# One edge buffer, sixteen output slots and one step a turn in a graph-layer kernel

## The chip, the core and the metric

The kernel runs on one core of one Trainium2 chip. The metric is the device time of one execution in microseconds. Five engines share the work: TensorE (PE in the profile, its weight loads PEld), VectorE (DVE), ScalarE (ACT), GpSimd (POOL) and SyncE (SP), which here only issues DMA transfers. The profile page comes from one profiled execution.

## What is computed

A layer over a graph with 12,500 nodes of 128 features and 412,500 edges of 48 features. The edges are sorted by `dst`, the node that receives them.

```python
recv = edge_index[1]
agg = jax.ops.segment_sum(edges, recv, num_segments=N_NODES)
u = graph_globals[batch]                      # batch is all zeros
x = jnp.concatenate([nodes, agg, u], axis=1)  # nodes = relu(layernorm(x))
h = jax.nn.relu(x @ W1 + b1)                  # 256 hidden
return h @ W2 + b2                            # added to the layer's input x
```

Everything is float32. The edge features are 79 MB of the 88 MB that are read, and 6.4 MB are written.

## The kernel before

**Edges.** A group is 128 x 7 = 896 edges. A step takes 19 groups, held as five quads (0 to 4: four times four groups, then three), so one step is 17,024 edges; there are 24 full steps and a last one of 5 groups. Quads 0 to 2 are part 0, quads 3 and 4 part 1. `edge_buf` exists twice, by the parity of the step: SyncE loads quad q of step s+2 (`load_quad`, L327) once TensorE has used quad q of step s (`edges_used`).

**Sums.** For each quad VectorE writes a one-hot matrix (`make_onehot`, L777) from `rel`, the receiver of each edge relative to its group's first, and TensorE multiplies it with the edges (`sum_quad`, L1020: 168 matmul records in part 0, 98 in part 1). ScalarE copies the sums (`copy_sums`), VectorE takes the low part (`low_sums`), TensorE moves them to their place in a window of nodes (`place`, L1043) with the help of `placing`, and VectorE adds the window to `agg` (`add_window`, L803). `rel` comes in four blocks of 128 groups: `relative` (L540), a turn on TensorE (`turn_rel`, L1004) and a copy (`copy_rel`, L549). Block 0 is made in the startup, blocks 1 to 3 in steps 2 to 7, between other work.

**Nodes.** Step s also carries one tile of 512 nodes through its stages: x of tile s is normalised (VectorE `moments`, `join_moments`, `invert` with the instruction `shift` L834; ScalarE `deviate`, `normalise`) and turned on TensorE (`turn_x`, L1058, then ScalarE `copy_turned`). For tile s-2 ScalarE copies `agg` into `tile_sums` (`tile_high`, L598), VectorE writes its low part (`tile_low`, L840), TensorE runs `first_layer` (w_node L1068, w_high L1072, w_low L1074) and `second_layer` (L1086), with `relu_hidden` on ScalarE between. For tile s-3 ScalarE copies the result and GpSimd adds x and b2 (`add_out`, L514) into `out_buf`; GpSimd's other work in a step is `x_plus_b2` (L502). `out_buf` has two slots; `add_out` waits until the tile before last is stored.

**Order.** Each engine runs a fixed list written by hand and semaphores join them. SyncE's list in step s: x of tile s+1, part 0 of step s+2, the store of tile s-4, part 1 of step s+2. All these transfers go through one queue. TensorE runs a loop of 12 turns with two steps in each; the other engines' lists are unrolled. After the last step VectorE checks that the input is sorted and within the windows, and adds the last two tiles' outputs itself; a general path behind a branch is taken only if a check fails.

## Time and profile before

| | us |
|---|---|
| median of 3 runs | 277.42 (277.35 to 277.61) |
| the profiled execution | 277.42 |
| its span in the trace | 275.7 |
| TensorE busy | 243.9 (88%) |
| VectorE busy | 241.4 (88%) |
| ScalarE busy | 146.3 (53%) |
| GpSimd busy | 75.4 (27%) |

The span runs from the first to the last instruction of the program; the 1.7 us more in the execution's time lie around it. The granted clock is the share of TensorE's full speed that the chip allows; there are two levels, 1.2 and 2.4 GHz, and the mean over the span was 0.961. Busy shares are means over a startup of some 40 us, a loop of steps and a tail of some 30 us, so a limit has to be read from a stage, not from the table. The page's line of GB/s has 40 slices of 6.9 us.

### The profile page before, as it was taken

What the parts mean: (1) busy time and instruction counts of PE and PEld (TensorE: products, weight loads), DVE (VectorE), ACT (ScalarE), POOL (GpSimd) and SP (SyncE); (2) the same over time, 40 slices, a digit from 0 to 9 for tenths busy, and PEclk for the clock granted to TensorE, in tenths of its full rate; (3) what the DMA queues carried; (4) which work ended last, traced back from release to release, by engine and by line L of the source; (5) the groups of instructions that cost most, each with busy time, mean ns of one, the idle gap of its engine ahead of it and who ended that gap; (6) DMA issues with size and microseconds to landing.
All of it is one profiled execution on the core that took longest, in us unless ns stands there. A gap on an engine that the chain in (4) does not pass through costs nothing.

```text
span 275.7 us, 17264 instructions
## 1 busy us (share of the span) xinstructions
PE 243.9 (88%) x7448; PEld 195.3 (71%) x7448; DVE 241.4 (88%) x579; ACT 146.3 (53%) x315; POOL 75.4 (27%) x89
## 2 busy tenths in 40 slices
PE   7344869989999999799999999999999998999893
PEld 5234757687787788588778778877887796787572
DVE  2977699979879998999999999999999999886394
ACT  3712156566577564556455555655565555456640
POOL 8473010402113203203302312311330330334210
PEclk9955599999999999999999999999999999999999
DMA  7999999999999999999999999999999999982101
GB/s 247 370 381 379 336 382 385 360 330 382 390 387 387 392 389 386 378 390 387 390 394 386 386 393 388 384 389 386 367 391 390 386 372 375 387 291 88 40 38 57
DMA packets 70876, 94.53 MB, mean 343 GB/s; under 512 B 4324, under 2 KB 64260, under 8 KB 70854
## 3 DMA queue, kind: packets, MB, share of 16 engines
q1 hardware_dynamic: 69802, 94.29, 95.6%
q10 hardware_dynamic: 956, 0.00, 0.2%
q8 instruction: 7, 0.11, 0.2%
q14 instruction: 15, 0.12, 0.1%
q0 software_dynamic: 96, 0.00, 0.0%
HBM read 87.88 MB, written 6.40 MB: 342 GB/s over the span
## 4 chain that ended last, share of the span: by engine, by line
DMA 60%; PE 16%; DVE 12%; issue 5%; SPq 2%; POOL 1%; ACT 0%; DVEq 0%; POOLq 0%
DMA out<-out_buf 56%; PE group_bank L1020 6%; DVE onehot L777 5%; DMA x_buf<-in_x 3%; PE out_bank L1086 3%; SPq L327 2%; PE hidden_bank L1068 2%; PE window_bank L1043 2%; DVE rel_rows L732 2%; POOL out_buf L514 1%; DMA dst_rows<-in_dst 1%; DVE tile_sums L840 1%; DVE bn L819 1%; PE hidden_bank L1004 1%; DVE placing L789 1%
## 5 line engine op out<-in xcount | busy, mean ns | idle before, releaser
L777 DVE TENSOR_TENSOR onehot<-rel,const_bank 128x896 f32<-128x896 f32 (+1 forms) x122 | 122.8, 1026 | 8.1 <-PE group_bank L1020 8.0
L1020 PE MATMUL group_bank<-edge_buf,onehot 128*32 128x48 f32 x6454 | 87.1, 211 | 9.9 <-DVE onehot L777 5.8
L1020 PEld LDWEIGHTS group_bank<-edge_buf,onehot 128*32 128x32 f32 x6454 | 79.9, 113 | 22.2 <-issue 12.3
L514 POOL TENSOR_TENSOR out_buf<-mlp_out,xb_buf 128x512 f32<-128x512 f32 x23 | 29.6, 1288 | 166.0 <-DMA out<-out_buf 137.1
L1068 PE MATMUL hidden_bank<-normed_t,w_node 128*128 128x512 f32 (+1 forms) x100 | 51.6, 597 | 0.8 <-issue 0.7
L1086 PE MATMUL out_bank<-w_sb,hidden 128*128 128x128 f32 x384 | 47.7, 277 | 1.4 <-ACT normed_t L587 1.4
L1086 PEld LDWEIGHTS out_bank<-w_sb,hidden 128*128 128x128 f32 x384 | 44.7, 192 | 1.6 <-issue 1.6
L576 ACT ACTIVATE normed_x<-x_buf,shift,inverse 128x128 f32<-128x128 f32 x98 | 40.3, 482 | 9.7 <-DVE shift L834 9.7
L1072 PE MATMUL hidden_bank<-tile_sums,w_high 112*128 112x512 f32 (+1 forms) x50 | 39.0, 781 | 0.0
L502 POOL TENSOR_TENSOR xb_buf<-x_buf,b_rows 128x512 f32<-128x512 f32 (+1 forms) x25 | 31.6, 1267 | 19.8 <-DMA x_buf<-in_x 10.3
L608 ACT ACTIVATE hidden<-hidden_bank,hidden_bias 128x512 f32<-128x512 f32 (+1 forms) x50 | 32.3, 670 | 4.3 <-PE hidden_bank L1074 4.2
L1043 PE MATMUL window_bank<-placing,sums_high 128*48 128x128 f32 (+3 forms) x122 | 23.0, 245 | 8.2 <-DVE sums_low L810 5.4
L803 DVE TENSOR_TENSOR agg<-agg,window_bank 48x352 f32 (+1 forms) x49 | 21.4, 438 | 8.4 <-PE window_bank L1043 6.9
L568 ACT ACTIVATE deviation<-mean_var,eps_col 128x4 f32<-128x4 f32 (+1 forms) x25 | 7.4, 298 | 38.5 <-DVE mean_var L825 38.5
L561 ACT ACTIVATE sums_high<-group_bank 128x96 fp32r<-128x96 f32 (+1 forms) x49 | 13.1, 267 | 27.2 <-PE group_bank L1020 24.8
L1043 PEld LDWEIGHTS window_bank<-placing,sums_high 128*48 128x48 f32 (+1 forms) x122 | 14.4, 125 | 14.5 <-DVE agg L803 7.0
L789 DVE TENSOR_TENSOR placing<-node_ramp,const_bank 128x456 fp32r<-128x456 f32 (+2 forms) x49 | 24.6, 504 | 0.0
L587 ACT ACTIVATE normed_t<-out_bank 128x512 f32<-128x512 f32 (+1 forms) x25 | 14.7, 588 | 17.3 <-PE out_bank L1058 17.3
L598 ACT ACTIVATE tile_sums<-agg 48x512 fp32r<-48x512 f32 (+1 forms) x25 | 15.6, 623 | 15.5 <-DVE agg L803 15.5
L819 DVE BATCH_NORM_STATS2 bn<-x_buf 128x6 f32<-128x128 f32 x98 | 21.4, 280 | 1.5 <-DMA x_buf<-in_x 0.9
L1043 PE MATMUL window_bank<-placing,sums_low 128*48 128x128 f32 (+3 forms) x122 | 21.6, 232 | 0.0
L840 DVE TENSOR_TENSOR tile_sums<-agg,tile_sums 48x512 fp32r<-48x512 f32 (+1 forms) x25 | 18.6, 744 | 1.8 <-ACT tile_sums L598 1.0
(92 smaller groups left out, 218.1 us busy)
## 6 DMA issues: line engine op xcount, KB each, us to landing
edge_buf<-in_edge_attr SPq DMA_DIRECT2D x97, 672.0 KB, 10.4
edge_buf<-in_edge_attr SPq DMA_DIRECT2D x24, 504.0 KB, 10.3
x_buf<-in_x SPq DMA_DIRECT2D x24, 256.0 KB, 8.9
out<-out_buf SPq DMA_DIRECT2D x23, 256.0 KB, 9.4
dst_rows<-in_dst SPq DMA_DIRECT2D x3, 448.5 KB, 7.8
dst_rows<-in_dst SPq DMA_DIRECT2D x1, 252.3 KB
out<-out_buf SPq DMA_DIRECT2D x1, 224.0 KB
edge_buf<-in_edge_attr SPq DMA_DIRECT2D x1, 168.0 KB, 9.2
```

What stands on the lines that cost most here:

```text
L502: pool.tensor_tensor(xb_buf[k.third][:, 0:nj, :], x_buf[k.parity][:, 0:nj, :], b2_rows[:, :].unsqueeze(1).to_broadcast([P, nj, F_NODE]), A ...
L514: pool.tensor_tensor(out_buf[k.parity][:, 0:nj, :], mlp_out[:, 0:nj, :], xb_buf[k.third][:, 0:nj, :], ALU.add).then_inc(out_added, 1)
L576: done = act.activation(normed_x[:, j, :], x_buf[k.parity][:, j, :], ACT.Relu, bias=shift[:, j:j + 1], scale=inverse[:, j:j + 1])
L608: act.activation(hidden[k.parity][:, c, 0:cols], hidden_bank[c][:, 0:cols], ACT.Relu, bias=hidden_bias[:, c:c + 1]).then_inc(hidden_copied, 1)
L777: dve.tensor_tensor(onehot[:, c0:c0 + cols, :], rel[:, r0:r0 + cols].unsqueeze(2).to_broadcast([P, cols, WINDOW]), ramp_const.unsqueeze(1) ...
L789: dve.tensor_tensor(placing[h][:, 0:nq, :, 0:width], node_ramp[:, :, 0:width].unsqueeze(1).to_broadcast([P, nq, NJ, width]), position_cons ...
L819: dve.bn_stats(bn6[:, j, :], x_buf[k.parity][:, j, :]).then_inc(moments_halfway, 1)
L1020: done = pe.matmul(group_bank[h][WINDOW * j:WINDOW * (j + 1), n * F_EDGE:(n + 1) * F_EDGE], onehot[:, (g0 + j) * EDGES_PER_ROW + r, :], ed ...
L1043: done = pe.matmul(bank[:, :, low // NJ:high // NJ], sums[h][0:rows, n, :], placing[h][0:rows, n, :, 0:(high - low) // NJ], start=(n + par ...
L1068: pe.matmul(hidden_bank[c][:, 0:cols], w1_node[:, c * P:(c + 1) * P], normed_t[k.parity][:, 0:cols], start=True, stop=False)
L1072: pe.matmul(hidden_bank[c][:, 0:cols], w1_high[:, c * P:(c + 1) * P], tile_sums[k.parity][:, 0:cols], start=False, stop=False)
L1086: done = pe.matmul(to_bank[:, j * P:(j + 1) * P], hidden[k.parity][:, c, j * P:(j + 1) * P], w2_sb[:, c, :], start=(c == 0), stop=(c == 1))
```

## The change

1. There is one `edge_buf`. Quad q of step s+1 is loaded into it once TensorE has used quad q of step s.
2. There are 16 slots of `out_buf`. SyncE stores tiles 0 to 8 in the steps 4, 6, ... 20, and tiles 9 to 22 after all loads.
3. `tile_low` of all tiles but the last three runs on GpSimd, ahead of `add_out`.
4. TensorE's loop has 24 turns of one step. In it `first_layer` comes ahead of `turn_x`; the first turns take other branches. `normed_t`, `hidden` and `tile_sums` use one buffer for all tiles but one near the end. `keep_clock` is a loop instead of a written-out list.
5. Startup: blocks 1 to 3 of `dst` are loaded ahead of x of tile 1 or right behind it, and `relative`, `turn_rel` and `copy_rel` of blocks 1 to 3 run before step 2. The instructions of `step_bases` on VectorE come later, and the base addresses for `add_window` are read into registers ahead of the last one-hot of a step.

The diff, cut to this:

```diff
-        self.value = c + 2 * i if self.static else i * 2 + c
+        self.value = i + c
@@ buffers
-        edge_buf = [sb(f"edge_buf{p}", [P, GROUPS, ROW]) for p in range(2)]
+        edge_buf = sb("edge_buf", [P, GROUPS, ROW])
-        out_buf = [sb(f"out_buf{p}", [P, NJ, F_NODE]) for p in range(2)]
+        out_buf = [sb(f"out_buf{n}", [P, NJ, F_NODE]) for n in range(OUT_SLOTS)]
+        def own(k):
+            return 1 if k.static and k.value == tiles - 2 else 0
+        def slot(k):
+            return k.value % OUT_SLOTS if k.static else 0
@@ SyncE
-                if not s.below(2):
-                    sp.wait_ge(edges_used, s.plus(-2).value * NQ + q + 1)
+                if not s.below(1):
+                    sp.wait_ge(edges_used, s.plus(-1).value * NQ + q + 1)
...
+            load_dst(1)
+            load_part(At(1), 0)
+            load_weights()
+            load_part(At(1), 1)
+            load_dst(2)
             load_x(At(1))
-            for s in range(steps):
...
+            load_dst(3)
+            for s in range(1, steps):
+                if s + 1 < steps:
+                    load_part(At(s + 1), 0)
+                if s < tiles - 1:
                     load_x(last_tile() if s + 1 == tiles - 1 else At(s + 1))
+                if s >= 4 and s % 2 == 0 and s // 2 - 2 < tiles - OUT_SLOTS:
+                    store(At(s // 2 - 2))
+                if s + 1 < steps:
+                    load_part(At(s + 1), 1)
+            for k in range(tiles - OUT_SLOTS, tiles - 2):
                 store(At(k))
@@ GpSimd
+            def tile_low(k):
+                pool.wait_ge(tile_high_ready, k.value + 1)
+                pool.tensor_tensor(sums_tile(k, STACK_LOW), agg_tile(k), sums_tile(k, 0).bitcast(fp32), ALU.subtract)\
+                    .then_inc(tile_low_ready, 1)
             for s in range(steps):
+                if 2 <= s < full_steps:
+                    pool.wait_ge(xb_ready, s)
+                    tile_low(At(s - 2))
+                    pool.wait_ge(tile_low_ready, s + 1)
@@ ScalarE
             copy_sums(At(0), 1)
+            relative(1)
             deviate(At(0))
             normalise(At(0))
+            copy_rel(1)
             copy_sums(At(1), 0)
             copy_turned(At(0))
+            bias()
             deviate(At(1))
+            relative(2)
             copy_sums(At(1), 1)
             normalise(At(1))
+            copy_rel(2)
+            relative(3)
+            copy_rel(3)
@@ VectorE
-                if s >= 2:
-                    tile_low(At(s - 2))
...
                 make_onehot(n, 3)
+                base = [window_base(At(s), h) for h in range(2)]
                 make_onehot(n, 4)
@@ TensorE
-            with pe.Fori(0, full_steps // 2) as i:
...
+            with pe.Fori(0, full_steps) as i:
+                step = At(0, i)
+                sum_part(step, 0)
+                with pe.If(i > 1):
+                    place(step.plus(-1), 1)
+                    pe.wait_ge(rel_ready, 2 * blocks)
+                    first_layer(step.plus(-2))
+                    turn_x(step.plus(-1))
+                with pe.Else():
+                    with pe.If(i > 0):
+                        place(At(0), 1)
+                        turn_x(At(0))
+                        sum_bias()
+                    with pe.Else():
+                        turn_places()
+                sum_part(step, 1)
+                place(step, 0)
+                with pe.If(i > 1):
+                    second_layer(step.plus(-2))
+                with pe.Else():
+                    pe.wait_ge(bias_ready, i * 2 + 1)
+                    turn_rel(i + 1)
+                    with pe.If(i > 0):
+                        turn_rel(3)
```

How instructions stand in a row, at the places that matter. SyncE's list in the middle of the loop, before: every step has its x, its quads and a store.

```order
L342 DMA x_buf<-in_x 128x512
L327 DMA edge_buf<-in_edge_attr 128x4x336 x3
L347 DMA out<-out_buf 128x512
L327 DMA edge_buf<-in_edge_attr 128x4x336
L327 DMA edge_buf<-in_edge_attr 128x3x336
```

The same of the changed kernel, two steps: the quads come ahead of x, and the store stands in every second step.

```order
L343 DMA edge_buf<-in_edge_attr 128x4x336 x3
L358 DMA x_buf<-in_x 128x512
L363 DMA out<-out_buf 128x512
L343 DMA edge_buf<-in_edge_attr 128x4x336
L343 DMA edge_buf<-in_edge_attr 128x3x336
L343 DMA edge_buf<-in_edge_attr 128x4x336 x3
L358 DMA x_buf<-in_x 128x512
L343 DMA edge_buf<-in_edge_attr 128x4x336
L343 DMA edge_buf<-in_edge_attr 128x3x336
```

ScalarE's list from part 1 of step 0 to the first `tile_high` (the copy into `tile_sums`), before.

```order
L561 ACTIVATE sums_high<-group_bank 128x96
L568 ACTIVATE deviation<-mean_var,eps_col 128x4
L576 ACTIVATE normed_x<-x_buf,shift,inverse 128x128 x4
L561 ACTIVATE sums_high<-group_bank 128x144
L587 ACTIVATE normed_t<-out_bank 128x512
L568 ACTIVATE deviation<-mean_var,eps_col 128x4
L561 ACTIVATE sums_high<-group_bank 128x96
L576 ACTIVATE normed_x<-x_buf,shift,inverse 128x128 x4
L598 ACTIVATE tile_sums<-agg 48x512
```

The end of that stretch in the changed kernel, from the sums of part 1 of step 1 on: the copy of block 2 of `rel`, the making of block 3 and its copy now stand between `normalise` of tile 1 and the first `tile_high`.

```order
L586 ACTIVATE sums_high<-group_bank 128x96
L601 ACTIVATE normed_x<-x_buf,shift,inverse 128x128 x4
L574 ACTIVATE rel<-hidden_bank 128x4x128
L574 ACTIVATE rel<-hidden_bank 128x3x128
L562 ACTIVATE neg_first<-dst_rows 77x1
L565 ACTIVATE rel_rows<-dst_rows,neg_first 77x896
L574 ACTIVATE rel<-hidden_bank 128x4x77
L574 ACTIVATE rel<-hidden_bank 128x3x77
L623 ACTIVATE tile_sums<-agg 48x512
```

## Rows read from the trace of the kernel before

**Rows 1.** The page, parts 1 and 2: busy us (share); GB/s in 40 slices

```profile
PE 243.9 (88%) x7448; PEld 195.3 (71%) x7448; DVE 241.4 (88%) x579; ACT 146.3 (53%) x315; POOL 75.4 (27%) x89
...
GB/s 247 370 381 379 336 382 385 360 330 382 390 387 387 392 389 386 378 390 387 390 394 386 386 393 388 384 389 386 367 391 390 386 372 375 387 291 88 40 38 57
```

**Rows 2.** Table by stretch: us, busy us (count) by engine, granted clock, DMA share, GB/s

```profile
68.78:244.44 175.66, 169.78 (x5488) 135.97 (x5487) 166.19 (x398) 99.70 (x223) 44.13 (x35) 1.00 1.06 386
205.42:214.85 9.43, 9.25 (x305) 7.45 (x304) 8.79 (x23) 5.29 (x12) 2.31 (x2) 1.00 1.07 388
15.00:36.00 21.00, 12.03 (x384) 10.64 (x384) 15.00 (x38) 3.63 (x10) 6.24 (x4) 0.51 1.07 366
```

**Rows 3.** Timeline, TensorE: start us, us, what, count [idle before]; steps 2, 3, 5, 23

```profile
37.02 2.00 PE L1020 MATMUL group_bank<-edge_buf,onehot 128*32 128x48 f32 x168 [0.42 <-issue]
...
47.84 1.99 PE L1020 MATMUL group_bank<-edge_buf,onehot 128*32 128x48 f32 x168
...
68.78 1.99 PE L1020 MATMUL group_bank<-edge_buf,onehot 128*32 128x48 f32 x168
...
244.44 1.99 PE L1020 MATMUL group_bank<-edge_buf,onehot 128*32 128x48 f32 x168
```

**Rows 4.** Timeline, TensorE, one step (19) and the next one's start

```profile
205.42 1.99 PE L1020 MATMUL group_bank<-edge_buf,onehot 128*32 128x48 f32 x168
...
208.79 0.80 PE L1072 MATMUL hidden_bank<-tile_sums,w_high 112*128 112x512 f32 x1
...
211.09 1.40 PE L1020 MATMUL group_bank<-edge_buf,onehot 128*32 128x48 f32 x98
...
214.85 0.55 PE L1020 MATMUL group_bank<-edge_buf,onehot 128*32 128x48 f32 x32
```

**Rows 5.** Timeline, VectorE, the same step

```profile
206.36 1.09 DVE L777 TENSOR_TENSOR onehot<-rel,const_bank 128x896 f32<-128x896 f32 x1 [0.55 <-PE group_bank L1020]
207.48 0.68 DVE L840 TENSOR_TENSOR tile_sums<-agg,tile_sums 48x512 fp32r<-48x512 f32 x1
...
212.48 0.16 DVE L834 SCALAR_TENSOR_TENSOR shift<-mean_var,inverse 128x4 f32<-128x4 f32 x1
```

**Rows 6.** Timelines of VectorE and GpSimd around 136 us

```profile
136.23 0.99 DVE L834 SCALAR_TENSOR_TENSOR shift<-mean_var,inverse 128x4 f32<-128x4 f32 x1
...
135.93 1.27 POOL L502 TENSOR_TENSOR xb_buf<-x_buf,b_rows 128x512 f32<-128x512 f32 x1
```

**Rows 7.** Groups by line, GpSimd: busy us, mean ns, idle before

```profile
L451 POOL TENSOR_TENSOR spread<-place_rel,ramp 25x640 f32<-25x640 f32 x1 | 1.3, 1252 | 0.1
```

**Rows 8.** DMA issues at 80 to 208 us (last column: landing), and the chain's first piece

```profile
edge_buf<-in_edge_attr SPq DMA_DIRECT2D x52, 672.0 KB, 10.4
...
0.83 3.27 DMA dst_rows<-in_dst
```

**Rows 9.** Timeline, SyncE, the last stores of whole tiles

```profile
247.04 19.05 SPq L347 DMA_DIRECT2D out<-out_buf  x4
```

**Rows 10.** Timeline, TensorE: start of the second part of step 0, and a turn_rel

```profile
15.85 2.46 PE L1020 MATMUL group_bank<-edge_buf,onehot 128*32 128x48 f32 x98 [4.49 <-DVE onehot L777]
...
57.96 1.02 PE L1004 MATMUL hidden_bank<-ident,rel_rows 128*128 128x128 f32 x7
```

**Rows 11.** Timeline, VectorE, startup

```profile
15.42 3.36 DVE L746 TENSOR_SCALAR step_base<-step_base_f 1x50 int32<-1x50 f32 x1
...
31.71 0.86 DVE L819 BATCH_NORM_STATS2 bn<-x_buf 128x6 f32<-128x128 f32 x4
```

**Rows 12.** Timeline, ScalarE, startup

```profile
36.18 1.65 ACT L576 ACTIVATE normed_x<-x_buf,shift,inverse 128x128 f32<-128x128 f32 x4 [1.05 <-DVE shift L834]
...
47.42 1.05 ACT L540 ACTIVATE rel_rows<-dst_rows,neg_first 128x896 f32<-128x896 int32 x1
...
58.65 1.87 ACT L549 ACTIVATE rel<-hidden_bank 128x512 f32<-128x512 f32 x2 [1.12 <-PE hidden_bank L1004]
```

**Rows 13.** DMA issues at 17.5 to 17.9 us, last column: us to landing

```profile
x_buf<-in_x SPq DMA_DIRECT2D x1, 256.0 KB, 7.7
```

More of the change, by code:

```diff
@@ L183, in gnn_kernel @@
         b2_in = sem("b2_in")
-        edges_in = [[sem(f"edges_in{p}{q}") for q in range(NQ)] for p in range(2)]
+        edges_in = [sem(f"edges_in{q}") for q in range(NQ)]
         x_in = [sem(f"x_in{p}") for p in range(2)]
-        stored = [sem(f"stored{p}") for p in range(2)]
+        stored = [sem(f"stored{n}") for n in range(OUT_SLOTS)]
         last_stored = sem("last_stored")
@@ L399, in _ @@
             store_last(last_tile(), last_stored)
-            sp.wait_ge(stored[0], 16 * (tiles // 2))
-            sp.wait_ge(stored[1], 16 * (tiles // 2) + 16)
+            for n in range(OUT_SLOTS):
+                sp.wait_ge(stored[n], stores_of(n) * 16)
             sp.wait_ge(last_stored, 16)
@@ L428, in _ @@
                 general_tiles(sp, tile)
-                sp.wait_ge(stored[0], 16 * (tiles // 2 + tiles))
+                sp.wait_ge(stored[0], 16 * (stores_of(0) + tiles))
         @block.gpsimd
@@ L602, in relu_hidden @@
                     act.wait_ge(out_ready, k.value)
-                elif not k.below(2):
-                    act.wait_ge(out_ready, k.value - 1)
+                elif not own(k):
+                    act.wait_ge(out_ready, before_own(k))
                 for c in range(2):
@@ L670, in _ @@
                     split_weights()
-                copy_turned(At(s - 1))
-                if s == 2:
-                    bias()
                 deviate(At(s))
                 relu_hidden(At(s - 2))
+                copy_turned(At(s - 1))
                 copy_sums(At(s), 1)
                 normalise(At(s))
-                if s % 2 == 1 and s // 2 < blocks:
-                    copy_rel(s // 2)
-                if s % 2 == 0 and s // 2 < blocks:
-                    relative(s // 2)
                 if s == 2 * blocks:
@@ L846, in last_out @@
                 dve.wait_ge(xb_ready, n)
-                dve.wait_ge(stored[k.parity], k.turn * 16)
-                dve.tensor_tensor(out_buf[k.parity][:, 0:nj, :],
+                dve.wait_ge(stored[slot(k)], k.value // OUT_SLOTS * 16)
+                dve.tensor_tensor(out_buf[slot(k)][:, 0:nj, :],
                                   bank[:, 0:nj * P].rearrange("p (j f) -> p j f", j=nj),
@@ L899, in _ @@
                 make_onehot(n, 2)
-                add_window(At(s - 1), 1)
+                add_window(At(s - 1), 1, base[1])
                 low_sums(At(s), 0)
@@ L915, in _ @@
             make_placing(At(steps - 1), 0)
+            last_base = window_base(At(steps - 1), 0)
+            dve.wait_ge(tile_low_ready, tiles - 3 + 2)
             tile_low(At(tiles - 3))
@@ L918, in _ @@
             invert(last)
-            add_window(At(full_steps - 1), 1)
+            add_window(At(full_steps - 1), 1, base[1])
             low_sums(At(steps - 1), 0)
-            add_window(At(steps - 1), 0)
+            add_window(At(steps - 1), 0, last_base)
             tile_low(second)
@@ L938, in _ @@
                 dve.sem_inc(general_added, 1)
-                dve.wait_ge(stored[0], 16 * (tiles // 2))
-                dve.wait_ge(stored[1], 16 * (tiles // 2) + 16)
+                for n in range(OUT_SLOTS):
+                    dve.wait_ge(stored[n], stores_of(n) * 16)
                 dve.wait_ge(last_stored, 16)
@@ L1105, in keep_clock @@
                 ones16 = ones[:, :].bitcast(mybir.dt.bfloat16)
-                for _ in range(n):
+                with pe.Fori(0, n):
                     pe.matmul(bank[:, 0:2 * P], ones16[:, 0:P], ones16[:, :], start=True, stop=True)
```

154 lines of the change are left out of this document (61 added, 93 removed).

## The prediction, made before the changed kernel was run

> **What bounds the kernel now.** I read the page first, then a table by stage, then one step engine by engine. The page has TensorE and VectorE both at 88% of the span, and the DMA at 330 to 394 GB/s until the last loads [rows 1]. A step is one turn over 19 groups (five quads) of edges, and the 18 steps between the 168-matmul rows at 68.78 and 244.44 take 175.66 us, 9.76 us each [rows 3]; in that stretch TensorE is busy 169.78 us, VectorE 166.19 us, and the DMA moves 386 GB/s [rows 2]. So three resources stand within 6% of one another, and the question is which ends last.
>
> TensorE's own step can be read where nothing disturbs it: it begins at 205.42, and the next at 214.85, 9.43 us [rows 4]. I take 9.4 us as its floor. In that step VectorE waited 0.55 us for TensorE [rows 5]. VectorE's floor there is therefore at most 9.43 - 0.55 = 8.9 us. Elsewhere it is longer: the same shift instruction that takes 0.16 us at 212.48 [rows 5] takes 0.99 us at 136.23, and it ends (137.22) as GpSimd's add of 135.93 ends (137.20) [rows 6]. Steps of 9.7 us are of that kind: VectorE is blocked by GpSimd for up to 0.8 us and then ends last. The DMA: a step reads 4 x 672 + 504 KB of edges and 256 KB of x and writes 256 KB, 3.79 MB, at 389 GB/s 9.75 us (388 in the clean step [rows 2]). The edges are not what anybody waits for: they are issued a whole buffer ahead, 10.4 us from issue to landing being queueing [rows 8], and a lone transfer needs 3.27 us for 448.5 KB [rows 8], so about 2.1 us beside its 1.2 us of data. The chain on the page, 56% out<-out_buf, shows the stores queued behind these loads; GpSimd waits for them, and that decides when its two adds run against VectorE.
>
> **The change, part by part.**
>
> Stores. 14 whole tiles are stored after the last load, 9 within the loop on alternate steps. A step's traffic falls to 3.53 MB (9.1 us at 389 GB/s), with a store 9.75 us, on average 9.4 us while stores are issued. The 14 tiles are 3.67 MB or 9.4 us of DMA; from the last load (about 242 us in the old trace) to the last output there are 30 us, in which the DMA is nearly idle [rows 1], so they cost nothing. SyncE's store of the next-to-last tiles waits for GpSimd's late add anyway (four stores over 19.05 us [rows 9]). If this cover were gone they would cost up to 9.4 us. The wait of GpSimd on a landed store goes: its adds then follow their inputs.
>
> tile_low (L840) to GpSimd. VectorE loses 0.68 us and two small gaps, 0.75 us a step, and stands at 8.2 us of a 9.4 us step. GpSimd's price is not in the trace. Its full-tile add takes 1.27 us for 128x512, one of 25x640 took 1.25 us [rows 6, 7]; I take 1.3 us for 48x512, with 0.7 (what VectorE takes) and 2.6 us (twice) as ends. Three operations of 1.3 us fit in a step. Who waits: TensorE's w_high matmul, 3.4 us after its step begins (205.42 to 208.79, rows 4), 2.9 us in the new order, in which first_layer goes ahead of turn_x. With VectorE early, add_window of the step ends at about TensorE's step start, ScalarE's copy takes 0.63 us, GpSimd 1.3: ready 2.1 us after the start, 0.8 us of slack; at 2.6 us it would cost 0.5 us a step. The remaining VectorE instruction that GpSimd blocked, the shift, comes 6.5 us into the step, and GpSimd's three operations should be over after 5.0 us. So the blocks of up to 0.83 us vanish; if they all stayed, VectorE would have 9.0 us, still under 9.4. The Trainium skill speaks against such a move (Perfetto Trace Analysis, "Optimizing Scalar/DVE Operations"): the two engines share a port, so that shifting work between them might not help; the Trainium skill's page SBUF — State Buffer, "SBUF: two separate sides", calls the port an exclusive lock that also binds a VectorE operation with two SBUF inputs. By that rule, the trace agrees [rows 6]; struck in every step it would leave VectorE at 9.0 us, and the sum as it is.
>
> One edge buffer. A quad's reload is issued when TensorE has used it, so it has a step less about 0.7 us to land. In steady state TensorE uses q0 at +0.65, q1 at +1.3, q2 at +2.0, q3 at +6.4, q4 at +7.0. Five loads and x, 9.1 us of data, go through a queue that is empty at first: q0 to q2 land by about +2.8 + 5.3 = +8.1 and x by +8.8, before the next step's +9.4 to +10.7; q3 and q4, issued at +6.5, land by +11.9, wanted at +15.1. So it starts with some 3 to 4 us of slack and loses 0.35 us with each store step, and gains 0.3 us in each other: it does not run out in 20 steps at 389 GB/s. Cost taken: 0.3 us in all; bounds 0 and 7 us (rival B).
>
> One step a turn. The step's matmuls are the same. The loop turns twice as often, but its branch is resolved while the matmuls of second_layer are still queued. I take 0; the bounds are -0.1 and +0.2 us a step, from the 9.43 us of rows 4 against the 9.25 us that TensorE was busy in it [rows 2]. window_base ahead of the last onehot: VectorE's sequencer does it while the engine has onehot q3, up to 0.3 us against 1.2 us of slack: 0.
>
> Startup. All three remaining blocks of rel (relative, turn_rel, copy_rel) now come before step 2, and nothing of them is left in the loop; before, 1.05 us and 1.87 us of ScalarE [rows 12] stood ahead of tile_high in steps 3 to 7. Step 2 began at 37.02, step 3 at 47.84: 10.82 us [rows 3]. What is late next is x of tile 1. It stands behind 8.9 MB (dst blocks, ten quads, weights); by the slices of 6.9 us on the page (247, 370, 381 and 379 GB/s [rows 1]) 6.9 MB of it have moved by 20.7 us and the rest by 26.1, with 2.1 us of latency 28.2, and I take 28.5 to 29; before, it was issued between 17.5 and 17.9 and took 7.7 us, so landed near 25.3 [rows 13]. From the start of moments(1) at 31.71 to that of normalise(1) at 36.18 it took 4.5 us [rows 11, 12]: shift ends about 33.5; normalise 1.65, copy_rel(2) 1.87 to 2.1, relative(3) 1.05 and its small first part 0.2, turn_rel(3) 1.0 us [rows 10, 12]: step 2 begins at about 39.5, **+2.5 us**. The 3.36 us that VectorE spends on a clamp of 1x50 elements at 15.42 [rows 11] go or shrink, but they lie before the landing of x and give nothing. In step 2 first_layer also waits for w1_low, since copy_rel(3), tile_high and split_weights stand ahead of it on ScalarE, 1.9 us for the first [rows 12] and by my estimate some 1.5 us for the rest, against the 2.4 us after which TensorE wants it: about **+1.0 us**. The clock: at 15 to 36 us it was granted 0.51 on average [rows 2], and 98 matmuls took 2.46 us in place of 1.40 [rows 4, 10]; the new idle stretches of 3 us before step 2 make it likely that part of step 2 runs at 1.2 GHz. I take **+1.0 us**, bounds 0 and 7.
>
> **The sum**, against the profiled execution's 275.7 us span. Up to step 2 +2.5; step 2 itself 9.4 in place of 10.82, -1.4, +1.0, +1.0; steps 3 to 22, 244.44 - 47.84 = 196.6 us before, 20 x 9.4 = 188.0 now, -8.6; DMA +0.3. From step 23 on (31.3 us) the work and its waits are the same: 0. Together -5.2 us, span 270.5. The profiled execution took 277.42 us as a whole, which is the median of the runs, so 277.4 - 5.2 = **272.2 us**.
>
> **Rivals.**
> A: the startup costs nothing, because the x load or ScalarE's chain is 3 us earlier than I think. Then -10.0 + 0.3: 267.7 us. For it: the 3.36 us of the clamp go [rows 11]. Against: x cannot land before its 8.9 MB.
> B (slower): the shallow queue. 389 GB/s was read with 10 us of transfers always queued; with one buffer at times only two quads are. If the rate falls to the 366 GB/s of the startup [rows 2], a step needs 9.65 us, with a store 10.35, on average 10.0: 20 steps cost 12 us more than at 9.4 less 4 us of initial slack, +8: 280 us. The sign turns where a mean step of 3.66 MB takes 9.86 us (20 x 0.46 - 4 = 5.2), at 371 GB/s. Against it: the queue never empties in my timing once the stores run.
> C: the clock stays down for a step or more after the idle stretch before step 2. A step at the ratio 2.46/1.40 costs 7 us more; -5.2 + 6: 278.2 us. The Trainium skill (TensorE: Matmul & The Clock Gate, "What's actually happening") says that idleness throttles the clock and activity releases it. By that rule, the trace agrees: 0.51 was granted where TensorE had stood idle for 4.49 us before 15.85 [rows 2, 10].
> D: VectorE or GpSimd ends last after all (tile_low at 2.6 us, 0.5 us a step): -5.2 + 10: 282 us; half of it, no change.
>
> **How the numbers follow.** My forecast (269.5 to 275.5) 0.60; A 0.14; B 0.09; C 0.08; D 0.04; a mixture near no change 0.05. The range is 268.2 to 277.3, which leaves out the lower half of A and most of B and D. Faster holds the forecast, A and half of C and of the mixture; slower holds B and the rest of C and D. About 0.2% is what a measurement of this kernel can tell from no change. Faster 0.81, same 0.06, slower 0.13.
>
> **What would show it.** In the changed trace: 168-matmul rows 9.4 us apart from step 3 on (9.7 or more refutes the floor or shows B, then TensorE waits for edge_buf); shift at 0.16 us throughout; GpSimd's tile_low at 1.3 us and no w_high matmul waiting for it; step 2 beginning at 39 to 40; the granted clock at 1.00 from about 43 us; PE's step 23 at about 239; the 14 stores over by 255, and a tail of 31 us. I am wrong if the loop is under 9.3 us a step, if step 2 is earlier than 37, or if the tail changes by more than 1 us.

## The result: 280.6 us, slower by 1.1%

| | before | after |
|---|---|---|
| time, median of four runs each | 277.5 us | 280.6 us (280.1 to 281.7) |
| ratio to before, 95% interval | | 1.011 [1.009, 1.014] |
| span of the profiled execution | 275.7 us | 278.1 us (as a whole 280.1) |
| step 2 begins | 37.02 us | 40.51 us |
| step 3 begins | 47.84 us | 52.28 us |
| steps 3 to 22 | 196.6 us | 194.63 us |
| from step 23 to the end | 31.3 us | 31.2 us |

The forecast was 272.2 us. The page of the changed kernel, parts 1 and 2, to be held against [rows 1]:

```profile
PE 249.7 (90%) x7448; PEld 200.0 (72%) x7448; DVE 218.8 (79%) x557; ACT 145.0 (52%) x315; POOL 103.1 (37%) x111
...
PEclk9977958999999999999999999999999999999998
DMA  7999958899999999999999999999999999999611
GB/s 250 368 364 341 336 182 273 271 387 365 388 384 384 386 378 388 366 380 345 379 359 370 388 380 338 390 379 386 380 366 382 378 357 387 369 333 380 257 40 57
```

VectorE went from 88% to 79% of the span, as intended, and TensorE stayed the busiest. The row that says something new is the last: from the ninth slice on, in the loop, five fall under 360 GB/s (345, 359, 338, 357, 333), where before one did. Two stretches in the table by stretch, the startup's second 20 us and the loop from step 3 to step 23 (us, busy us and count of TensorE, its weight loads, VectorE, ScalarE, GpSimd, then granted clock, DMA share, GB/s):

```profile
20.00:40.00 20.00, 10.98 (x307) 9.85 (x306) 12.87 (x35) 11.83 (x25) 3.65 (x3) 0.75 0.97 309
...
52.28:246.91 194.63, 188.62 (x6082) 152.72 (x6081) 166.47 (x424) 104.65 (x240) 76.57 (x60) 1.00 1.06 374
```

374 GB/s stand against 386 of before [rows 2]. TensorE's timeline shows where the time lies. These rows are the last transpose before step 2, steps 2 and 3, the wait inside step 2, and the beginnings of steps 6 and 23 (here and below, a row with a count under 168 is cut off by the end of the window asked for; only its start matters):

```profile
38.80 1.77 PE L1036 MATMUL hidden_bank<-ident,rel_rows 128*128 128x128 f32 x7 [2.31 <-ACT rel_rows L565]
40.51 3.46 PE L1051 MATMUL group_bank<-edge_buf,onehot 128*32 128x48 f32 x168
...
45.30 1.12 PE L1098 MATMUL hidden_bank<-normed_t,w_node 128*128 128x512 f32 x2 [0.97 <-issue]
...
52.28 1.91 PE L1051 MATMUL group_bank<-edge_buf,onehot 128*32 128x48 f32 x160
...
80.29 0.92 PE L1051 MATMUL group_bank<-edge_buf,onehot 128*32 128x48 f32 x66
...
246.91 0.80 PE L1051 MATMUL group_bank<-edge_buf,onehot 128*32 128x48 f32 x55
```

Steps 3 to 5 take 28.01 us, 9.34 us each: the floor of 9.4 us is there. From step 6 to step 23 it is 166.62 us for 17 steps, 9.80 us each. Up to step 20 a step of 9.35 us mostly stands between longer ones of 9.6 to 10.5, but not strictly: 9 and 10, and 16 and 17, are both longer, and so are 20, 21 and 22, the last two of which have no store. This is one of the long ones, step 14, and the beginnings of 15 and 16, on TensorE:

```profile
158.44 1.40 PE L1051 MATMUL group_bank<-edge_buf,onehot 128*32 128x48 f32 x112
160.68 0.80 PE L1051 MATMUL group_bank<-edge_buf,onehot 128*32 128x48 f32 x56 [0.85 <-DMA edge_buf<-in_edge_attr]
...
165.16 1.39 PE L1051 MATMUL group_bank<-edge_buf,onehot 128*32 128x48 f32 x98
...
168.85 1.99 PE L1051 MATMUL group_bank<-edge_buf,onehot 128*32 128x48 f32 x168
...
178.21 1.99 PE L1051 MATMUL group_bank<-edge_buf,onehot 128*32 128x48 f32 x140
```

After 112 matmuls (quads q0 and q1) TensorE stands still for 0.85 us: quad q2 has not landed. From step 3 to step 23 TensorE waits for edges 3.6 us in 6 places and for a one-hot 1.2 us in 2; in the same steps VectorE waits for the x that stands behind q2, 4.7 us in 8 places. The rest of the 7.8 us over 20 steps of 9.34 lies in shorter waits that were not followed. No row with a wait for edge_buf exists in the loop of before.

### The profile page after: what moved, and what is told of

It reads as the page before. It is cut to its first block, busy times and chain, and to the rows that moved or that the text cites. A ratio compares the mean times of both kernels' runs of the same rounds, so it can differ in the third digit from the quotient of the medians.

```text
span 278.1 us, 17414 instructions
## 1 busy us (share of the span) xinstructions
PE 249.7 (90%) x7448; PEld 200.0 (72%) x7448; DVE 218.8 (79%) x557; ACT 145.0 (52%) x315; POOL 103.1 (37%) x111
## 4 chain that ended last, share of the span: by engine, by line
PE 62%; DMA 23%; DVE 7%; issue 3%; ACT 2%; POOL 1%; SPq 1%; DVEq 0%; POOLq 0%
PE group_bank L1051 22%; DMA edge_buf<-in_edge_attr 20%; PE hidden_bank L1098 12%; PE out_bank L1116 11%; PE window_bank L1073 6%; PE hidden_bank L1102 3%; PE hidden_bank L1104 3%; DMA x_buf<-in_x 3%; PE out_bank L1088 3%; DVE onehot L804 2%; PE window_bank L1138 2%; DVE rel_rows L759 2%; PE hidden_bank L1036 1%; ACT normed_x L601 1%; ACT rel L574 1%
## 5 line engine op out<-in xcount | busy, mean ns | idle before, releaser
L804 DVE TENSOR_TENSOR onehot<-rel,const_bank 128x896 f32<-128x896 f32 (+1 forms) x122 | 125.4, 1030 | 29.7 <-PE group_bank L1051 22.1
L1051 PE MATMUL group_bank<-edge_buf,onehot 128*32 128x48 f32 x6454 | 89.1, 211 | 6.4 <-DMA edge_buf<-in_edge_attr 3.6
L535 POOL TENSOR_TENSOR tile_sums<-agg,tile_sums 48x512 fp32r<-48x512 f32 x22 | 28.1, 1277 | 133.1 <-ACT tile_sums L623 133.1
L1098 PE MATMUL hidden_bank<-normed_t,w_node 128*128 128x512 f32 (+1 forms) x100 | 52.7, 608 | 1.1 <-issue 1.0
L633 ACT ACTIVATE hidden<-hidden_bank,hidden_bias 128x512 f32<-128x512 f32 (+1 forms) x50 | 33.5, 671 | 13.3 <-PE hidden_bank L1104 13.3
L623 ACT ACTIVATE tile_sums<-agg 48x512 fp32r<-48x512 f32 (+1 forms) x25 | 15.6, 624 | 13.8 <-DVE agg L833 13.8
L1098 PEld LDWEIGHTS hidden_bank<-normed_t,w_node 128*128 128x128 f32 x100 | 16.9, 189 | 4.7 <-issue 1.1
## 6 DMA issues: line engine op xcount, KB each, us to landing
edge_buf<-in_edge_attr SPq DMA_DIRECT2D x1, 168.0 KB, 6.7
```

Of the source, the lines that this page charges most:

```text
L535: pool.tensor_tensor(sums_tile(k, STACK_LOW), agg_tile(k), sums_tile(k, 0).bitcast(fp32), ALU.subtract)\
L633: act.activation(hidden[own(k)][:, c, 0:cols], hidden_bank[c][:, 0:cols], ACT.Relu, bias=hidden_bias[:, c:c + 1]).then_inc(hidden_copied, 1)
L804: dve.tensor_tensor(onehot[:, c0:c0 + cols, :], rel[:, r0:r0 + cols].unsqueeze(2).to_broadcast([P, cols, WINDOW]), ramp_const.unsqueeze(1) ...
L1051: done = pe.matmul(group_bank[h][WINDOW * j:WINDOW * (j + 1), n * F_EDGE:(n + 1) * F_EDGE], onehot[:, (g0 + j) * EDGES_PER_ROW + r, :], ed ...
L1098: pe.matmul(hidden_bank[c][:, 0:cols], w1_node[:, c * P:(c + 1) * P], normed_t[own(k)][:, 0:cols], start=True, stop=False)
```

## Why the loads came late

SyncE's timeline in the same step:

```profile
159.30 2.61 SPq L343 DMA_DIRECT2D edge_buf<-in_edge_attr  x3
162.01 0.85 SPq L358 DMA_DIRECT2D x_buf<-in_x  x1
162.90 0.43 SPq L363 DMA_DIRECT2D out<-out_buf  x1
166.03 5.44 SPq L343 DMA_DIRECT2D edge_buf<-in_edge_attr  x5
```

With one buffer the loads leave SyncE in two bursts: q0, q1, q2, x and a store between 159.3 and 163.3, then nothing for 2.7 us, because q3 and q4 are not free until TensorE reaches them at 165.16. From the issue rows and the DMA packets of the trace I worked out what had been issued and not yet moved, and the rate in half microseconds (the last row leaves out q0 of the next step, whose issue runs from 169.72 to 170.08):

```
at us   issued, not moved   rate over the next 0.5 us
163.5        1.96 MB             382 GB/s
165.0        1.39                384
166.0        1.02                384     (q3, q4 issued now)
167.0        1.84                367
168.0        1.46                262
168.5        1.33                256
169.0        1.20                299
170.0        0.89                358
```

At 168.0 there are 1.46 MB outstanding and the rate is down to two thirds. Of these 1.46 MB, 1.2 MB are q3 and q4, issued at most 2 us earlier, and a load needs, by my estimate, about 2 us before it moves anything (a lone one took 3.27 us for 1.2 us of data [rows 8]). What was issued before the gap has nearly run out.

It runs out unevenly. A load is done when its semaphore has had 16 updates, one from each DMA engine, and the trace has each update's time. For q2 of step 14 the first came at 157.75, the ninth at 158.28 and the last at 160.56. TensorE started at 160.68, 2.4 us after half the engines had delivered. The Trainium skill (DMA: Bandwidth & Descriptors, "Why a DMA increments its semaphore by 16 and not by 1") says that the semaphore climbs by one as each engine's data lands, and that only the full 16 mean that all has landed; the trace agrees. In the changed kernel first and last were about 2.8 us apart in the loop, in the kernel before 4.6 us. There nobody waited for it; its loads landed 10.4 us after their issue [rows 8], here 7.5:

```profile
edge_buf<-in_edge_attr SPq DMA_DIRECT2D x52, 672.0 KB, 7.5
```

(DMA issues at 80 to 208 us; the last column is the median from issue to landing, in us.) So with one buffer, I concluded, a fast engine runs dry in the gap between the bursts while a slow one still holds up the quad that TensorE wants. This is argued, not shown: the packets in the trace don't tell the engines apart. Between 100 and 240 us, 25 of 280 half microseconds are under 330 GB/s in the changed kernel, 5 in the kernel before. Packets of over 150 ns (the median is 58) number 240 and 66. That was the theory; what follows tested it against others. I call it Q (the queue), since how far ahead the loads stand is what it says matters.

## Experiments

### One buffer alone, in the kernel before

```diff
-        edge_buf = [sb(f"edge_buf{p}", [P, GROUPS, ROW]) for p in range(2)]
+        edge_buf = [sb("edge_buf", [P, GROUPS, ROW])] * 2
...
-                if not s.below(2):
-                    sp.wait_ge(edges_used, s.plus(-2).value * NQ + q + 1)
+                if not s.below(1):
+                    sp.wait_ge(edges_used, s.plus(-1).value * NQ + q + 1)
```

The order of the loads follows the changed kernel too: the quads ahead of x in every step, and dst and the weights as in its startup.

> The kernel before, with one part of the change alone: one edge buffer, a quad's reload issued when TensorE has used the quad of the step before, and SyncE's loads in the order that this needs. Stores in every step, VectorE, GpSimd, ScalarE and TensorE's loop as before. Theory Q (the queue): with one buffer 7 us of loads stand in the queue in place of 10, and every stall of one of the 16 DMA rings then holds up a load that TensorE waits for; the rate falls from 386 GB/s to 360 to 375, a step of 3.79 MB takes 10.1 to 10.5 us in place of 9.76, 18 steps cost 6 to 13 us more: 284 to 291 us. Theory W (the rate fell because the stores of the changed kernel lie differently, not because of the buffer): 386 GB/s stay, 277.5 us, plus at most 2 us from the startup.

Measured: 285.4 us, ratio 1.031 [1.028, 1.035]; the profiled execution was the shortest of the four, 283.02 us. Slower as Q said, but for more than Q's reason. The table by stretch, in its first half and its second:

```profile
90.00:130.00 40.00, 36.49 (x1210) 28.79 (x1208) 35.80 (x87) 21.32 (x48) 11.52 (x8) 1.00 1.03 362
170.00:210.00 40.00, 38.91 (x1228) 31.14 (x1228) 36.60 (x91) 22.33 (x51) 10.19 (x8) 1.00 1.07 386
```

The rate is 362 GB/s in the first and 386 in the second, at 9.7 to 9.9 us a step, about what 3.79 MB take at that rate. So one buffer can carry 386 GB/s when every step is alike and DMA ends last, and Q's 360 to 375 GB/s is not borne out there; TensorE then waits 1.9 us for edges in 7 places between 150 and 250 us. In the first half TensorE waits for no edges at all, but for VectorE, and VectorE is held up by GpSimd. VectorE's row and then GpSimd's, from their timelines:

```profile
103.14 1.72 DVE L841 TENSOR_TENSOR tile_sums<-agg,tile_sums 48x512 fp32r<-48x512 f32 x1
```

```profile
103.04 1.27 POOL L515 TENSOR_TENSOR out_buf<-mlp_out,xb_buf 128x512 f32<-128x512 f32 x1 [8.29 <-ACT mlp_out L617]
```

tile_low takes 1.72 us in place of 0.69; of the first eleven, six take 1.35 us or more, in the kernel before two of all. GpSimd's add waited for ScalarE here, no longer for a store, and fell onto VectorE's instruction. The size of this run's loss is thus partly a collision that the changed kernel, with tile_low on GpSimd, does not have. Steps 3 to 8 take 10.56 us each here, 10.12 in the kernel before.

### Only the low tile sums on GpSimd, in the kernel before

```diff
-                if s >= 2:
-                    tile_low(At(s - 2))
...
+                if 2 <= s < full_steps:
+                    pool.wait_ge(xb_ready, s)
+                    tile_low(At(s - 2))
```

> The kernel before, with only the low tile sums moved from VectorE to GpSimd. If the DMA's 3.79 MB a step at 386 to 389 GB/s set the step of 9.76 us, this changes nothing: 277.5 us, within 0.5. If VectorE, blocked by GpSimd's adds, ended last (as the prediction had it), 20 steps fall towards TensorE's 9.4 us: up to 6.6 us less, 271 us; half of that would be 274.

Measured: 277.8 us, ratio 1.003 [1.001, 1.005]. VectorE is relieved and nothing is gained, at 386 GB/s (100 to 240 us):

```profile
100.00:240.00 140.00, 133.42 (x4272) 106.04 (x4272) 117.57 (x307) 76.33 (x172) 54.34 (x43) 1.00 1.07 386
```

From step 3 to step 23 it took 196.56 us, the kernel before 196.6. Something is gained at first and given back: steps 8 to 13 take 9.39 us each, steps 14 to 22 then 9.98, with 3.79 MB at 386 GB/s 9.83. The second buffer lets TensorE run ahead of the DMA for a while; over the whole loop the bytes set the time, not VectorE's blocked instructions.

### No stores in the loop

```diff
-                if s >= 4 and s % 2 == 0 and s // 2 - 2 < tiles - OUT_SLOTS:
-                    store(At(s // 2 - 2))
```

Nine tiles of the output are never written.

> The changed kernel without the nine stores in its loop (nine tiles of the output are never written). Every step then moves 3.53 MB. Steps without a store took 9.35 us and those with one about 10.3 us, so if the store itself is what is late, steps 6 to 23 take 17 x 9.35 = 159 us in place of 166.6: 273.0 us. If the whole loop runs at 373 GB/s whatever it moves, a step takes 9.46 us and the time is 275. If something else than DMA (the loop's branch, GpSimd) makes the alternate steps long, it stays at 280.

Measured: 275.35 us, ratio 0.994 [0.992, 0.995]. Steps 3 and 23 begin at

```profile
52.74 0.96 PE L1046 MATMUL group_bank<-edge_buf,onehot 128*32 128x48 f32 x70
...
240.72 0.46 PE L1046 MATMUL group_bank<-edge_buf,onehot 128*32 128x48 f32 x24
```

187.98 us, what the prediction had for them without its 0.3 (in the shortest of the four executions, 274.25 us). The branch, GpSimd and the order of the step cost nothing that shows. This does not say why a store costs more than its bytes.

### Two buffers, and two buffers held back

Two kernels differ from each other in how early a load may be issued. Both are the changed kernel with two edge buffers, two steps a turn and a constant tile in place of the output slots that no longer fit. The first loads a whole buffer ahead. The second has the same memory and waits as one buffer must. Its list on SyncE is also the changed kernel's: no quads of step 2 in the startup, and x behind the first three quads of a step, where the first has it ahead of them:

```diff
-                if not s.below(2):
-                    sp.wait_ge(edges_used, s.plus(-2).value * NQ + q + 1)
+                if not s.below(1):
+                    sp.wait_ge(edges_used, s.plus(-1).value * NQ + q + 1)
```

> The changed kernel with two edge buffers again and the loads a whole buffer ahead; TensorE's loop is written two steps a turn, which the two buffers need. The same nine stores in the loop and 14 behind it, but they send a constant tile, since there is no room for 16 slots (the output is not the reference's). Theory Q (the queue): 10 us of loads in flight, 386 to 389 GB/s, a mean step of 3.66 MB takes 9.4 us, steps 6 to 23 take 160 us in place of 166.6: 274 us. Theory W (a store beside these loads costs 1.35 us in place of 0.67): the alternate steps stay at 10.3 us or the mean at 9.8, 280 us.

> The kernel with two edge buffers of the earlier run, but with each quad's load held back until TensorE has used the same quad of the step before, as one buffer would need, and SyncE's loads in the changed kernel's order. Memory, loop form, stores (of a constant tile) and all engines' work stay as with two buffers; only how far ahead the loads are issued differs. Theory Q (how far ahead the loads stand): the loop falls back from 187.3 us (steps 3 to 23) to 193 to 196 and loads land 7 to 8 us after their issue: 280 us, give or take 1.5, since step 3 may begin earlier than at 55.2. Rival M (a load into memory that TensorE has just read, or the loop with one step a turn, is what costs): it stays at 187.3, 275.5 us.

Measured: 275.5 us with two buffers, ratio 0.994 [0.991, 0.996]; 281.8 us held back, 1.017 [1.015, 1.019]. Steps 3 and 23 of the first, then of the second:

```profile
55.17 1.02 PE L1050 MATMUL group_bank<-edge_buf,onehot 128*32 128x48 f32 x76
...
242.46 0.74 PE L1050 MATMUL group_bank<-edge_buf,onehot 128*32 128x48 f32 x49
```

```profile
54.22 0.97 PE L1048 MATMUL group_bank<-edge_buf,onehot 128*32 128x48 f32 x72
...
247.85 0.85 PE L1048 MATMUL group_bank<-edge_buf,onehot 128*32 128x48 f32 x60
```

187.3 us against 193.6, with the same stores. The issues at 80 to 208 us, first and second, show 10.2 and 7.5 us to landing:

```profile
edge_buf<-in_edge_attr SPq DMA_DIRECT2D x53, 672.0 KB, 10.2
```

```profile
edge_buf<-in_edge_attr SPq DMA_DIRECT2D x52, 672.0 KB, 7.5
```

This is the pair that decides. Memory that TensorE has just read, the loop's form and the stores are the same in both; what differs is the time of issue, with the place of x in the list that goes with it (not tried apart), and it is worth 6.3 us of span in the loop. With two buffers the 16 updates lie 4.4 us apart and TensorE never waits for an edge quad between 60 and 240 us; held back, they lie 2.7 us apart and it waits 4.5 us in 7 places.

The tables by stretch, up to step 3 and from step 3 to step 23, first kernel and then second, say what the 6.3 us are made of:

```profile
0.00:55.17 55.17, 38.67 (x915) 29.19 (x915) 32.88 (x78) 26.47 (x46) 19.16 (x45) 0.78 1.01 341
55.17:242.46 187.29, 185.69 (x6081) 151.25 (x6080) 165.09 (x423) 104.31 (x240) 76.58 (x60) 1.00 1.06 381
```

```profile
0.00:54.22 54.22, 38.36 (x915) 29.39 (x915) 33.04 (x78) 26.58 (x46) 19.14 (x45) 0.81 0.89 287
54.22:247.85 193.63, 187.62 (x6081) 152.06 (x6080) 166.32 (x424) 104.65 (x240) 76.52 (x60) 1.00 1.06 376
```

Time by rate gives the bytes. Up to step 3 the first kernel has moved 18.8 MB, the second 15.6; in the loop the first moves 71.4 MB at 381 GB/s, the second 72.8 at 376. By my estimate the lower rate is worth 2.5 of the 6.3 us (72.8 MB at 376 in place of 381), and 3.8 us are the 1.4 MB that the first kernel need not move in the loop. It lives on a stock: a mean step of 3.66 MB at 381 GB/s needs 9.61 us, and the steps take 9.31 up to step 20. In step 4 a quad stands landed 10 to 12 us before TensorE uses it, in step 22 2.6 to 4.0 us, and step 21 takes 10.19 us, with VectorE waiting 1.57 us for its x. In a longer loop the first kernel too would come to 9.61 us a step.

The two-buffer loop with nine stores is as short as the one-buffer loop with none, so nothing here says that a store costs more than its bytes; the stock would hide some of it.

### The small load out of the loop

```diff
             load_ends(0)
+            load_ends(1)
...
-                if s == 2 * blocks:
-                    load_ends(1)
```

> The changed kernel with one thing moved: ScalarE's small load of 478 four-byte elements (ends_i, the second half), which it issues in step 8 at 106.9 us, is issued at the start instead. In the changed kernel the 16 completions of one load stand 1.9 us apart from first to last before it and 3.1 us after it, and the steps that wait for an edge quad become longer from there on (9.7 before, up to 10.5 after). Theory Q1 (TensorE waits for the slowest of 16 DMA rings, so what delays one ring costs time when only 7 us of loads are queued): the distance stays below 2 us until another disturbance, and the loop is 2 to 4 us shorter: 276.5 to 278.5. Theory Q2 (only the total depth of the queue counts): 280.6, no change.

Measured: 280.6 us, ratio 1.009 [1.006, 1.013], no change from the changed kernel. The distance between first and last update went from 2.0 to 3.1 us at 106 us in the changed kernel; here it stayed between 1.9 and 2.4 us from 90 to 145 us and then went to 3.0 as well. The loop took 193.2 us in the profile and step 3 began 1.9 us later. What sets the engines apart is not this load alone; Q1, as worded for this run, is not borne out in the time. What drives them apart stays open.

### The stores on another queue

```diff
-                if s >= 4 and s % 2 == 0 and s // 2 - 2 < tiles - OUT_SLOTS:
-                    store(At(s // 2 - 2))
...
+                if s >= 4 and s % 2 == 0 and s // 2 - 2 < tiles - OUT_SLOTS:
+                    k = At(s // 2 - 2)
+                    act.wait_ge(out_added, k.value + 1)
+                    act.dma_start(out[bass.ds(tile_node0(k), TILE), :].rearrange("(p j) f -> p j f", j=NJ),
+                                  out_buf[slot(k)][:, :, :]).then_inc(stored[slot(k)], 16)
```

> The changed kernel with the nine stores of its loop issued by ScalarE at the end of the step, on a DMA queue of its own, in place of SyncE's between x and the next loads. If the store costs time because it stands in the one queue ahead of the loads of q3 and q4, that goes: the loop falls by up to 6 us, 275 us. If the 16 rings simply have nothing else queued when the store's packets and the first quads are done (Q), or the bytes are what counts, the alternate steps stay near 10.3 us: 280.5, within 1.

Measured: 279.5 us, ratio 1.006 [1.004, 1.008]. The loop took 193.75 us in place of 194.63, and its long steps were still 10.0 to 10.5 us. The Trainium skill (Perfetto Trace Analysis, "DMA Optimizations") advises one issuing engine for inputs and another for outputs; here that is worth about 1 us of the 6, with intervals of the two ratios that just touch. The store's place in SyncE's queue is a small part of the matter.

### x of tile 1 ahead of the weights

```diff
             load_part(At(1), 0)
+            load_x(At(1))
             load_weights()
             load_part(At(1), 1)
             load_dst(2)
-            load_x(At(1))
             load_dst(3)
```

> The changed kernel with x of tile 1 loaded before the weights and the second part of step 1, in place of after them and a block of dst. VectorE waited 1.8 us for this x at 29.78 and the last instruction of the chain from there sets the start of step 2 at 40.51. If that wait is what made the startup late, step 2 begins 2 to 3.5 us earlier (37 to 38.5), and the time is 277.5 to 278.5. If ScalarE's row of rel blocks and sums sets it anyway, step 2 stays at 40 and the time at 280.5. If the loop is held by the DMA, which moves the same bytes from the same start, part of the gain is given back there.

Measured: 277.75 us, ratio 1.001 [0.999, 1.004]. Step 2 begins at

```profile
38.17 1.11 PE L1051 MATMUL group_bank<-edge_buf,onehot 128*32 128x48 f32 x44
```

in place of 40.51, step 3 at 50.03 in place of 52.28, and the loop keeps its 194.1 us. So the landing of this x was late next in the startup, as the prediction said, and is worth 2.3 us of it.

### 23 slots, and the repairs together

dst_rows is free once dst has been tested for order. With the tests in steps 3 to 6 its memory holds seven more output tiles, and two stores are left in the loop:

```diff
-OUT_SLOTS = 16
+OUT_SLOTS = 23
+OWN_SLOTS = 16
...
+        old_dst = dst_rows[:, :, :].rearrange("p b e -> p (b e)")
+        out_buf += [old_dst[:, n * TILE:(n + 1) * TILE].bitcast(fp32).rearrange("p (j f) -> p j f", j=NJ)
+                    for n in range(OUT_SLOTS - OWN_SLOTS)]
```

> The changed kernel with 23 output slots: seven of them lie in the memory of dst_rows, which is free once VectorE has tested dst for order, in steps 3 to 6 in place of behind the loop. Only two tiles are stored in the loop, 21 behind the last load; the output is complete. The kernel without the loop's stores took 275.35 us; with two stores more and the tests off the tail I expect 275 to 275.8. If the 21 stores (5.4 MB, 14 us at 388 GB/s) are not hidden in the 31 us of the tail, or VectorE has no room for the tests, it is more than 277.

Measured: 274.2 us, ratio 0.987 [0.983, 0.990]. The loop takes 190.0 us; four steps with a test take 9.7 to 9.9 us each. The tail is 30.3 us.

> Put together from the kernel before: its two steps a turn and its startup of ScalarE, VectorE and TensorE (two blocks of rel inside the loop), with one edge buffer, the low tile sums on GpSimd and 23 output slots, seven in dst_rows. With one buffer alone step 3 began at 48.18 us, as before (47.84). If the loop runs at TensorE's 9.4 us once no store shares it: 48.2 + 188 + 31.3 us, and 1.7 around the span: 269 us. If instead the order of the old loop costs 9.6 us a step, 273. If the slow first half of the kernel with one buffer (10.3 us a step, VectorE's tile_low of 1.72 us under GpSimd's add) was the buffer and not that collision, it shows here too, 5 us more.

Measured: 276.5 us, ratio 0.996 [0.995, 0.997], far from the 269 of its expectation. Step 3 begins at 49.04 us, but the four steps from 108.80 to 149.81 us, with the tests in them, take 10.0 to 10.3 us each, and VectorE waits for the tests' completion one by one. The six steps from 49.04 to 108.80 us take 9.96 us each, as in the kernel before with only the low tile sums moved (9.97, with two buffers and a store in most steps): with the rel blocks among them they are slow whatever the buffer. From 149.81 on ten steps take 93.87 us, 9.39 each, again TensorE's floor once no store shares the loop.

The early x, the 23 slots, and the tests put ahead of the onehot that waits for TensorE, in the changed kernel:

> The changed kernel with both repairs: x of tile 1 ahead of the weights, and 23 output slots, seven in dst_rows; the tests of dst in steps 3 to 6 stand ahead of the onehot that waits for TensorE and are no longer waited for one by one. Step 3 at 50.0 us as with the early x, 20 steps of 9.35 to 9.4 us (187 to 188), a tail of 30.3 us as with 23 slots, 1.7 us around the span: 269 to 270.5 us. If VectorE has no room for the tests (9.7 us in those four steps, as before) 271.5. If the early x only moves the waiting into the loop, 274.

Measured: 272.1 us (271.4 to 274.7 in six runs), ratio 0.981 [0.980, 0.982]. It beats both kernels, with the whole output. It is about 2 us above its expectation. The profiled execution was the slowest of the six, 274.65 us; steps 3 and 23 begin at

```profile
50.11 1.09 PE L1062 MATMUL group_bank<-edge_buf,onehot 128*32 128x48 f32 x83
...
242.57 0.63 PE L1062 MATMUL group_bank<-edge_buf,onehot 128*32 128x48 f32 x40
```

192.5 us and not 187 to 188, with single steps of 10.5 and 10.2 us (from 118.07 and 185.31) long after the last store of the loop. One buffer with 3.53 MB a step needs about 9.2 us (between the landings of the same quad in the changed kernel's steps without a store), against a floor of 9.35: a margin of 0.1 us. Any quad that is late costs time, and nothing wins it back.

## Why the prediction was wrong, step by step

| step | predicted | measured |
|---|---|---|
| start of step 2 | 39.5, +2.5 | 40.51, +3.5 |
| step 2 | 11.4 | 11.77 |
| floor of a step | 9.4 | 9.32 to 9.35 |
| steps 3 to 22, with DMA | 188.3 | 194.63 |
| step 23 to the end | 31.3 | 31.2 |
| span | 270.5 | 278.1 |

The miss is 7.6 us of span: 1.3 by the start of step 3, 6.3 in the loop.

**The step that failed** is "One edge buffer": "it does not run out in 20 steps at 389 GB/s. Cost taken: 0.3 us in all; bounds 0 and 7 us". It was 6.6 us against the forecast's 9.4 us a step, near the upper bound, and 7.8 against the 9.34 that were measured. Two of its terms were wrong.

The rate was 374 GB/s and not 389. Only a part of that is the distance at which loads are issued: with two buffers this loop ran at 381, held back at 376. By my estimate 3.1 of the 6.6 us would have come at 381 GB/s too (72.8 MB in 191.1 us, where the forecast had 188.0), and 3.5 come from 374 in place of 381. Why the loop with two buffers stays under the 386 of before was not tried.

The slack was small. The forecast started with "some 3 to 4 us". For the quads of step 4, from the last of the 16 updates to TensorE's first matmul on them, it was 2.3, 2.2, 1.0, 1.0 and 2.3 us, and for q2 0.1 us from step 6 on. The forecast reasoned with one queue whose work is the sum of its bytes, where a quad has landed when the slowest of 16 engines has delivered, 2.3 us after the middle one in the step shown. In the kernels with two buffers a stock of landed quads paid for a rate below need; the forecast's 3 to 4 us were to do the same here.

**Rival B**, "the shallow queue", names what came, a lower rate with one buffer, and its 280 us is the time measured, but the number is partly luck. With 374 GB/s put in for its 366, its own sum gives 276 us; the other 4 us are the slack, which was less than its 4 us, and 1.3 us more of startup. Its turning point of 371 GB/s is for the same reason too low: the kernel was already slower at 374. It was given 0.09, on the argument that "the queue never empties in my timing once the stores run". It need not empty as a whole to lose a third of its rate for 1.5 us. The turning point stood only 5% under the 389 that the forecast counted on.

**VectorE in the kernel before.** The prediction read steps of 9.7 us as VectorE's, blocked by GpSimd. With tile_low on GpSimd and everything else as before, single steps fell to 9.39 us and later ones rose, and the 20 steps took the same time: over the loop they were the DMA's, 3.79 MB at 386 GB/s. This did not spoil the sum, since the changed kernel's bytes were counted apart, but it was wrong.

**The startup** was right in kind. x of tile 1 was late next: VectorE's bn waited 1.81 us for it and began at 29.78, some 1 us later than I had allowed, and the early x gave 2.3 us back. In step 2 the clock granted was 0.54 from 40.51 to 43.97 us, nearly all at 1.2 GHz, after TensorE had stood idle for 2.31 us before 38.80: 168 matmuls in 3.46 us in place of 1.99 (+1.5, forecast 1.0). From 43.97 on it was 1.00, so rival C did not come. first_layer waited 0.97 us (forecast 1.0).

**The rest held.** The floor of TensorE's step; the tail; GpSimd's price for tile_low, 1277 ns against a forecast of 1.3 us, with hardly a wait behind it (0.2 us in all before w_high's weights). The groups by line, GpSimd:

```profile
L535 POOL TENSOR_TENSOR tile_sums<-agg,tile_sums 48x512 fp32r<-48x512 f32 x22 | 28.1, 1277 | 133.1 <-ACT tile_sums L623 133.1
```

The shift that took 0.99 us at 136.23 before [rows 6] has a mean of 0.21 us over its 24 executions on a whole tile, 0.17 at most between 25 us and 250 us. GpSimd waits no more for a landed store.

## What to carry to other kernels

Memory taken from a load buffer is paid in two ways. The stock goes: a second buffer filled before the loop lets the loop run for a while faster than its DMA can feed it, here 18 steps, and one buffer does not. And the loads are issued later: before giving up the second buffer, compare the time from issue to need with the time to the last of the 16 completions, and add the gap between bursts of issues. A rate read from another kernel, with other bytes in a step and loads a buffer ahead, is not this one's. When bytes over rate is within a few per cent of the floor of the engine it feeds, a forecast of "hidden" is worth little: find the turning point and ask what would move the rate past it.

## What was not expected of the hardware

- The 16 completions of one 672 KB load lie 1 to 5 us apart, and further where loads are far ahead: 4.6 us in the kernel before, 4.4 with two buffers, 2.8 in the changed kernel, about 1 us in the first half of the kernel before with one buffer. When nobody waits for the last engine this costs nothing. The cause of the drift was not found; a small load moved out of the loop did not end it.
- One buffer is not always bound to the lower rate: the kernel before with one buffer moved 386 GB/s in its second half, with a store in every step and completions 2.3 to 3 us apart. Why the changed kernel, with steps of unequal bytes, did not reach that, and why the same loop with two buffers stayed at 381, was not tried.
- With the same 16 engines and the same bytes, packets of over 150 ns number 66 where the loads are far ahead (75 with two buffers) and 240 in the changed kernel (178 held back), between 100 and 240 us. They are no measure of lost time: the kernel without stores in the loop has 150, that with 23 slots 181, and the old loop with 23 slots 272, with steps at TensorE's floor in most of that stretch. Whether they are a sign of loads that begin on an idle engine was not tried.
